# Spreading a prefix layer normalization between matmul groups, doubling a convolution accumulator, and broadcasting a decay row by DMA, in an eight-core Mamba layer

## The reference

```python
xn = layernorm(x)
z, xBC, dt = split(xn @ W_in.T, [4096, 4096 + 6144])
xBC = silu(causal_depthwise_conv4(xBC))            # x 1024, B 1024, C 4096
dt = softplus(dt + dt_bias); A = -exp(A_log)       # 64 heads of width 64, state 128
y = chunked_scan(x, dt, A, B, C) + D * x           # state carried along the sequence
y = groupnorm_rms(y * silu(z)) * norm_weight
s = y @ W_out.T
h = fwht(xn * SU_ug); u = (h @ W_up.T) * su; t = (h @ W_gate.T) * sg
g = (fwht(silu(t) * u * SU_dp) @ W_down.T) * sd
out = x + s * silu(g)
```

## Time and profile before

| | us |
|---|---|
| three runs | 11702.4, 11736.15, 11411.93 |
| median | 11702.4 |
| the profiled execution | 11459.71 |
| span of its slowest core (core 0) | 11458.2 |
| spans of the eight cores | 11376.4 to 11458.2 |
| TensorE matmul busy | 6727.8 (59%) |
| VectorE busy | 3217.6 (28%) |
| ScalarE busy | 1905.7 (17%) |
| mean granted TensorE clock, core 0 | 0.743 |

### The profile page before, as it was taken

How to read it: one execution, slowest core, us unless ns; L and a number is a source line. 1 busy time by engine, 2 the same in 40 slices (tenths; PEclk the granted TensorE clock), 3 DMA queues, 4 the chain that set the end, 5 groups by cost and what they waited for, 6 DMA issues and landing times.

```text
span 11458.2 us, 102614 instructions; the slowest of 8 cores (11376.4 to 11458.2 us)
## 1 busy us (share of the span) xinstructions
PE 6727.8 (59%) x29866; PEld 2939.9 (26%) x30407; DVE 3217.6 (28%) x3926; ACT 1905.7 (17%) x2660; POOL 503.1 (4%) x884
## 2 busy tenths in 40 slices
PE   4445444556655445947887787732222259895793
PEld 2212111222222222413333333311111114341241
DVE  2120101044454554541111111144554520001302
ACT  2121212011111111311111111111111130304000
POOL 0000000000000000000000000011101110100000
PEclk8667676777777677978888888865555559896785
DMA  5222222212211111211111111113323333434124
GB/s 133 86 98 90 88 80 82 87 31 50 50 42 40 26 43 28 58 25 44 39 39 43 41 39 41 42 60 87 85 79 84 84 112 83 117 83 137 39 69 157
DMA packets 278273, 785.04 MB, mean 69 GB/s; under 512 B 49790, under 2 KB 132990, under 8 KB 251006
## 3 DMA queue, kind: packets, MB, share of 16 engines
q0 software_dynamic: 75024, 307.29, 13.6%
q1 hardware_dynamic: 202734, 471.16, 11.8%
HBM read 818.67 MB, written 162.01 MB: 86 GB/s over the span
## 4 chain that ended last, share of the span: by engine, by line
PE 48%; DVE 20%; DMA 13%; ACT 10%; issue 6%; SPq 1%; DVEq 1%; ACTq 0%; POOL 0%; another core or an unknown queue 0%; POOLq 0%
PE ps L950 9%; PE ps L1438 8%; PE ps L962 8%; PE ps L515 8%; PE ps L792 7%; PE ps L1565 4%; DMA WPF<-wpfx_scr 3%; DVE ACCP L673 3%; DVE XWG L722 2%; DMA dcc_scr<-DCC 2%; DVE ACC L832 2%; PE ps L739 1%; ACT X2H L1420 1%; DVE HPB L980 1%; DMA lnU_c<-u_pfx 1%
## 5 line engine op out<-in xcount | busy, mean ns | idle before, releaser
L792 PE MATMUL ps<-XN,WB 128*128 128x512 bf16 (+1 forms) x6286 | 1251.4, 362 | 403.6 <-ACT XBR L810 246.9
L515 PE MATMUL ps<-XNP,WPF 128*128 128x512 bf16 x3001 | 846.0, 447 | 556.9 <-DMA WPF<-wpfx_scr 499.6
L950 PE MATMUL ps<-XN,WUP 128*128 128x512 bf16 x4016 | 1045.0, 416 | 127.2 <-DMA WUP<-wup_blk 120.9
L962 PE MATMUL ps<-XN,WGT 128*128 128x512 bf16 x4012 | 919.5, 379 | 4.4
L1438 PE MATMUL ps<-X2H,WDB 128*128 128x512 bf16 x4014 | 894.2, 383 | 12.4 <-ACT X2H L1420 7.9
L792 PEld LDWEIGHTS ps<-XN,WB 128*128 128x128 bf16 x6400 | 605.9, 103 | 1060.2 <-issue 493.7
L980 DVE SCALAR_TENSOR_TENSOR HPB<-GTT,SUDP,UPT 128x512 bf16<-128x512 bf16 x256 | 192.3, 751 | 1576.8 <-ACT GTT L976 1576.8
L950 PEld LDWEIGHTS ps<-XN,WUP 128*128 128x128 bf16 x4096 | 431.3, 106 | 699.2 <-issue 302.6
L515 PEld LDWEIGHTS ps<-XNP,WPF 128*128 128x128 bf16 x3072 | 334.0, 111 | 1068.7 <-issue 831.1
L1438 PEld LDWEIGHTS ps<-X2H,WDB 128*128 128x128 bf16 x4096 | 404.0, 99 | 502.5 <-issue 46.9
L962 PEld LDWEIGHTS ps<-XN,WGT 128*128 128x128 bf16 x4096 | 400.8, 98 | 483.3
(11 more groups left out here) (179 smaller groups left out, 6619.0 us busy)
## 6 DMA issues: line engine op xcount, KB each, us to landing
CSREP<-csm_scr SPq DMA_DIRECT2D x64, 1024.0 KB, 4.7
WDB<-wdown_blk POOLq DMA_DIRECT2D x32, 2048.0 KB, 13.1
lnU_c<-u_pfx SPq DMA_DIRECT2D x48, 1024.0 KB, 6.0
WPF<-wpfx_scr POOLq DMA_DIRECT2D x88, 512.0 KB, 4.2
WPF<-wpfx_scr SPq DMA_DIRECT2D x88, 512.0 KB, 4.8
WB<-win_blk POOLq DMA_DIRECT2D x80, 512.0 KB, 6.0
WUP<-wup_blk POOLq DMA_DIRECT2D x64, 512.0 KB, 5.1
WGT<-wgate_blk POOLq DMA_DIRECT2D x64, 512.0 KB, 7.0
```

Source lines behind the costliest of these rows:

```text
L515: ins = t.matmul(PS[bank][0:mrows, :], lhs, XNP[pc][:, k, :], start=(k == 0), stop=(k == 15))
L792: ins = t.matmul(PS[bank][0:mrows, 0:w], lhs, XN[:, k, o:o + w], start=(k == 0), stop=(k == 15))
L950: ins = t.matmul(PS[bU][:, :], WUP[p][:, k, :], X1[:, k, s4 * 512:(s4 + 1) * 512], start=(k == 0), stop=(k == 15))
L962: ins = t.matmul(PS[bG][:, :], WGT[p][:, k, :], X1[:, k, s4 * 512:(s4 + 1) * 512], start=(k == 0), stop=(k == 15))
```

## The change

It has four parts.

- In the prefix stage a layer normalization call now takes one tile, and the calls are queued: after groups 2, 5, 8, 11, 14 and 16 (counted from 0) of each chunk one is taken, first of the four tiles for the next chunk but one, then of the core's own 17 tiles. The eight tiles for chunks 0 and 1 still come ahead of chunk 0.
- The decay column is read back by one broadcasting DMA to all 128 partitions (`DCBB`), and VectorE copies from that, in the prefix stage and in the scan stage. The rows `DCROW` and `DCROW6`, both matmuls and their PSUM banks' use are gone.
- The accumulator `ACCP` of the prefix convolution becomes two, used in turn.
- The generator has two more yields per block, one behind the convolution and one behind the state updates: 12 steps a block, 72 in all.

```diff
+from collections import deque
+        DCBB = sb("DCBB", [128, 64], BF16)
...
-            def emit_lnc(c):
+            def lnc_steps(c):
                 pc = c % 2
-                lnv[c] = ln_c(d_upfx, c * LCP, LCP // 128, XNP[pc], 0,
-                              dst_guard=ln_guard[pc])
+                steps = []
+                for tix in range(LCP // 128):
+                    def f(c=c, pc=pc, tix=tix):
+                        tokl = ln_c(d_upfx, c * LCP + tix * 128, 1, XNP[pc], tix,
+                                    dst_guard=ln_guard[pc])
+                        if tix == LCP // 128 - 1:
+                            lnv[c] = tokl
+                    steps.append(f)
+                return steps
 
             main_pos = [0]
 
-            def emit_main_ln(n):
-                if n > 0:
-                    ln_c(d_u, main_pos[0] * 128, n, XN, main_pos[0])
-                    main_pos[0] += n
-
-            def emit_mms(c):
+            def main_step():
+                def f():
+                    ln_c(d_u, main_pos[0] * 128, 1, XN, main_pos[0])
+                    main_pos[0] += 1
+                return f
+
+            def emit_mms(c, pending, mains):
...
-                for mi in [16] + list(range(16)):
+                for idx, mi in enumerate([16] + list(range(16))):
...
                     last_mm = tMM
+                    if idx in (2, 5, 8, 11, 14, 16):
+                        if pending:
+                            pending.popleft()()
+                        elif mains:
+                            mains.popleft()()
...
-                wDC1 = dma("sync", DCROW[:], dcc_scr.rearrange("a b -> b a"),
-                           waits=wl)
-                wl = [wDC1]
-                if bank_tok[4] is not None:
-                    wl.append(bank_tok[4])
-                tDC = op("tensor", lambda t: t.matmul(
-                    PS[4][:, 0:64], ONES1[:], DCROW[:], start=True, stop=True),
-                    waits=wl, inc=True)
-                dcrow_prev[0] = tDC
-                bank_tok[4] = op("vector", lambda v, cp=cp: v.tensor_copy(
-                    DCBA[:, cp, :], PS[4][:, 0:64]), waits=[tDC])
-
-            main_plan = [3, 3, 3, 3, 3, 2, 0, 0, 0, 0, 0, 0]
-            emit_lnc(0)
-            emit_lnc(1)
+                wDB = dma("sync", DCBB[:],
+                          dcc_scr.rearrange("a b -> b a").broadcast_to([128, 64]),
+                          waits=wl)
+                dcbb_prev[0] = op("vector", lambda v, cp=cp: v.tensor_copy(
+                    DCBA[:, cp, :], DCBB[:]), waits=[wDB])
+
+            for f in lnc_steps(0) + lnc_steps(1):
+                f()
+            pending = deque()
+            mains = deque(main_step() for _ in range(TL // 128))
             for c in range(NCHP):
-                emit_mms(c)
+                emit_mms(c, pending, mains)
                 if c % 2 == 1:
                     emit_dt(c // 2)
-                emit_main_ln(main_plan[c])
                 if c + 2 < NCHP:
-                    emit_lnc(c + 2)
+                    pending.extend(lnc_steps(c + 2))
+            while mains:
+                mains.popleft()()
             barrier()
...
-            ACCP = sb3("ACCP", [128, LCPB], F32)
+            ACCP = [sb3(f"ACCP{i}", [128, LCPB], F32) for i in range(2)]
...
                     for mi in range(16):
+                        ap = mi % 2
                         wl = [ldt[mi]]
-                        if vConvDone:
-                            wl.append(vConvDone[-1])
-                        elif conv_prev[0] is not None:
-                            wl.append(conv_prev[0])
+                        if accp_g[ap] is not None:
+                            wl.append(accp_g[ap])
...
+                        accp_g[ap] = vConvDone[-1]
                         if mi % 4 == 3:
                             yield
-                    conv_prev[0] = vConvDone[-1]
+                    yield
...
                         if gb % 2 == 1:
                             yield
+                    yield
                     ld_guard[:] = [last_st, vCl]
...
-                wD1 = dma("sync", DCROW6[:], dcc_scr.rearrange("a b -> b a"), waits=wl)
-                wl = [wD1] + ([bank_tok[5]] if bank_tok[5] else [])
-                tDC = op("tensor", lambda t: t.matmul(
-                    PS[5][:, 0:64], ONES1[:], DCROW6[:], start=True, stop=True),
-                    waits=wl, inc=True)
-                dcrow_prev = tDC
-                vDCB = op("vector", lambda v: v.tensor_copy(DCB6[:], PS[5][:, 0:64]),
-                          waits=[tDC])
-                bank_tok[5] = vDCB
+                wDB6 = dma("sync", DCBB[:],
+                           dcc_scr.rearrange("a b -> b a").broadcast_to([128, 64]),
+                           waits=wl)
+                vDCB = op("vector", lambda v: v.tensor_copy(DCB6[:], DCBB[:]),
+                          waits=[wDB6])
```

29 lines of the change are left out of this document (14 added, 15 removed).

## The result

The changed kernel is slower: the ratio of its time to the time of the kernel before is 1.032, with a 95% interval of 1.019 to 1.045, which just leaves open whether it is slower by 2%. Over all executions the medians are 11,928 us (8 of them) and 11,704 us (10, the kernel before), a ratio of 1.019; the profiled executions took 11,715.7 us and 11,459.7.

What follows compares the result with a forecast made beforehand. Stages taken as bounded by chains of waits, priced on TensorE: 484 - 4 - 7 + 0 - 114 + 31 = +390 us on 11459.7, so 11,850, 3.4% slower (12,092 on the median); range about 11,740 to 12,290.

Steps and rivals of the forecast that it cites:

- 8.0, near the 8.4: Prefix stage: assumed us from a one-tile row load's issue to its landing, with 6.0 and 9.6 kept for the range.
- cold restart: Prefix stage: TensorE's matmuls run slower after a gap, 2.6 us charged at each of 22 steps.
- from 408 us: Prefix stage sign: the transposes' waits for normalized tiles rise from 408 us to above 800.
- stands of 31 to 35 us: Prefix stage, after odd chunks: TensorE waits 31.2 us for weight tile 0, queued behind the decay column's store and load.
- I take 0, the end it is nearer to: Scan stage: the broadcasting load's effect over 13 exposed chunks, between -7 and +34 us, taken as 0.
- rival D: Broadcasting load lengthens its wait by 2.6 us in 13 chunks and 5 chains: +47, 11,897 us; 0.68 together with the forecast.
- the company of the fourth block's first convolution step: Projection stage: that step now runs beside the main convolution, costing about 5 us.
- an empty one costs nothing: Projection stage: an added resting place without prefix work only replaces weight tiles at the end that were free already.
- A: Prefix stage: row loads hide under running groups, only transposes cost TensorE, 145 us instead of 502; 11,009 us; chance 0.05.
- B: Prefix stage: shorter chain, loads landing in 6.0 us and no cold restart, 171 us less; 11,679 us, +1.9%; chance 0.12.
- C: Prefix stage: transfers collide, row loads land in 9.6 us and delay weight tiles, 178 us more; 12,028 us; chance 0.15.
- The few us that the start was to give: Ahead of chunk 0: the eight tiles' chains start a little sooner, -4 us.

Runs made afterwards that it cites:

- e2: The kernel before with only the one-tile normalization calls between weight groups; prefix stage 2516 us on core 4, +349.
- e3: The kernel before with only the broadcasting load of the decay row; ratio 1.002 (0.995 to 1.009), prefix stage on average 28 us more.
- e1: The changed kernel with normalization calls back in runs of three and four tiles behind each chunk; prefix 2194 to 2220 us, fastest execution 11,426 us.
- e4: The kernel before with only two accumulators in the prefix convolution, still ten steps a block; ratio 0.980 (0.968 to 0.991).
- e5: The kernel before with two accumulators and twelve steps a block; projection stage 2680 us on average, ratio 0.984 (0.971 to 0.997).
- e7: The changed kernel with each normalization step cut in three: load of tile i, sums and scaling of i-1, transposes of i-2; prefix 1935 us on average, ratio 0.998.
- e8: e7 with the decay column's store issued behind group 3 of the next chunk and its broadcasting load behind group 6; prefix 1893 us, ratio 0.972.
- e10: The kernel before with only its decay row made on TensorE from a diagonal, without store or load; prefix 2053, scan 1618, fastest execution 11,244 us.
- e12: e8 with decay row made on TensorE, state weights' store moved, four prefix weight buffers loaded two groups ahead, ten steps a block; prefix 985, fastest 9,921 us.

## Why the prediction was right, step by step

The forecast was slower: +390 us, or 3.4%. The measured ratio is 1.032; in us it is +224 by the medians (11,928, where 12,092 was forecast), +256 by the profiled executions and +321 in the touched stages. The changed kernel is slower for the reason given. The closeness of the sum is in part luck: part 1 was put 135 us too high, parts 2 and 4 together 54 too low.

- **Part 1** was put at +484 and costs 349 (e2). The mechanism is as written: load behind the store, transposes ahead of the group, TensorE standing for the whole chain. Two terms were mis-sized by much. The load "8.0, near the 8.4": its median landing is 5.3 us for the 40 prefix rows between groups and 6.7 for the 17 local ones, and a step is 18.2 and not 19.6, 80 us in all. And the "cold restart" of 2.6 us behind 22 steps does not exist: the matmuls after a step take 7.3 us for 31, and the stage's busy time is unchanged, 57 us. I had priced the restart from a gap in which TensorE did nothing, where here 16 transposes run at its end; whether these are the reason was not tried. 484 - 80 - 57 = 347. The waits of e2 show that the 80 are themselves what two larger errors leave: the waits for tiles grew by 494 us where the prediction's terms give 57 x (17.05 - 6.25) = 616, 122 too many, and the weight waits that run under a step are 24 and not 29, worth 147 us and not 188, 41 too many the other way. And the sign "from 408 us" took in the eight tiles ahead of chunk 0; the sum does not use it.
- **Part 2** was put at -7 and 0. In the prefix stage the stands of 31 to 35 us are the ones predicted (31.2), for the reason given, and with part 1 the net is nil (e2). Without part 1 it costs 28 (e3), for the longer way to the row loads behind it. In the scan stage "I take 0, the end it is nearer to" failed: +37 with the whole change, +52 in e1. That is rival D, which had 34 of its 47 us there; I had chosen the nearer row, of a 128 byte load, for one that fills 128 partitions.
- **Part 3** was put at -114 and is -115 (e4). In the later half a step gains 3.3 us (3.8 expected), 40 in all where 46 were expected; the earlier half gives the rest, more than its 68.
- **Part 4** was put at +31 and costs 41 (e5): the company of the fourth block's first convolution step was 8 and not 5, and "an empty one costs nothing" left out the 9 us behind the convolutions.
- **The rivals.** A needed the landing hidden, and e7 shows that it would then have had the direction right: the prefix stage is 233 us shorter, of A's 357. The order of the queues, not the idea, was missing. B was right on both of its terms, the 6.0 us and the restart, and its 11,679 is nearer to the measured 11,715.7 than my 11,850, but only by the 61 us of the untouched stages, without which the changed kernel would have taken 11,777; the ratio, +3.2%, lies by my forecast. C is out: the row loads landed sooner, not later, than I took.
- **The sum** of the corrected terms on the profiled scale is 349 + 37 - 115 + 41 = +312, against +321 in the touched stages. The few us that the start was to give, -4, are there as -5.

Behind the two rules of the prediction. The Trainium skill, "DMA: Bandwidth & Descriptors", Issuing engines are not separate DMA queues, has the transfers that ScalarE, SyncE and GpSimd start run on the same 16 DMA engines and interleave, and from that the prediction took a landing well above 6.0 us. e8 agrees with the rule itself, a tile from GpSimd landing after 22.9 us behind a store from SyncE; the size does not follow from it, and the measurement decides, for 5.3 and 6.7 us with a weight tile issued half a microsecond behind. By "Perfetto Trace Analysis", Optimization Strategy, of the Trainium skill, interleaving could have gained; with the order of e7 the runs agree, with that of the change they don't.

What I did not see, though the earlier trace rows have the 14.8 us of the column's store, is that it holds back the transfers issued behind it, of either engine.

## What to carry to other kernels

Spreading work between groups only hides it if each piece is cut where it waits, and the parts are issued a step apart; a chain that is kept whole and put between two matmul groups makes TensorE stand for all of it, where three or four in a row would have overlapped each other. Before replacing a wait, look at what stands behind the waiting DMA in its queue. A small value that must go to all partitions is made on TensorE from a diagonal in about 1 us; through DRAM it cost some 15 us and delayed its neighbours.

## What the runs showed of the hardware

- The store of a 64x1 column of bfloat16, 128 bytes from 64 partitions, takes a median of 10.9 us to land, up to 17 (the changed kernel). A 512 KB load issued from the same engine 3.5 us after it took 23.4 us where its median is 4.9, and one issued from GpSimd 22.9 where its median is 4.3 (e8). Slab loads of 64 KB from GpSimd take 2.1 to 3.8 us ahead of the first store of the scan stage and 8.9 to 12.4 within 4 us behind a store, in one and the same trace (kernel before); without the store their median is 2.2 (e10).
  The Trainium skill, "DMA: Bandwidth & Descriptors", Latency and other measured facts, puts the fixed cost of a transfer at about 2 us; for this store the runs have five times that. The same page, Rules for kernel authors, has one descriptor for each element where the last dimension is not contiguous; that this is the reason, no run here shows.
- The load of that column to 128 partitions, 16 KB, lands in a median of 5.7 us, as long as a 1 MB prefix row load from the same queue (5.7, both in the changed kernel); the 1x64 row was there with its matmul after 3.4.
- One core's transfers reached 195 GB/s over a whole stage (e12), beside 78 in the changed kernel.
